# Layer 0's offset stage: depthwise convolution in four 64x64 tiles, with the channel mean folded into its weights

## Chip, cores and metric

The kernel runs on one NeuronCore of a Trainium2 chip. The metric is the time of one execution on the device, in microseconds. Before the change the median of three runs is 1776.24 us (1775.21 to 1776.89).

## What is computed

The reference applies four layers to x (4 images, 64 channels, 48 x 48 pixels), each to a normalised x and added back to x. The change touches the first part of the first layer (the change's short title calls it layer 1, the code calls it layer 0), a deformable convolution:

```python
x_proj = x_nhwc @ w_in + b_in
x1 = conv_general_dilated(x, dw_w, ..., feature_group_count=C)      # 3x3, depthwise
x1 = x1.transpose(0, 2, 3, 1) + dw_b
mu = x1.mean(-1, keepdims=True)
var = ((x1 - mu) ** 2).mean(-1, keepdims=True)
x1 = (x1 - mu) * jax.lax.rsqrt(var + EPS) * ln_g + ln_b
x1 = jax.nn.gelu(x1, approximate=False)
offset = x1 @ w_off + b_off
mask = softmax((x1 @ w_mask + b_mask).reshape(N, H, W, G, P))
```

Mean and variance run over the 64 channels of one pixel. The stage that is changed, `offsets0`, makes `x_proj` and the raw offsets and mask values (`om`, 108 columns per pixel). What follows it in the kernel starts only when all of it is there.

## The kernel before

x lies in SBUF with 128 partitions: the lower 64 are the channels of images 0 and 1, the upper 64 those of images 2 and 3; the columns are two images side by side (`b2` is 0 or 1). `xp` is the same with a border of zeros. A chunk is 8 rows of 48 pixels, 384 columns, in both halves of the partitions at once, so the stage has 12 chunks (6 for each `b2`).

`vector_setup` (L142 to L164) runs ahead of the stage. VectorE makes `dwdiag` there (L154): for each of the nine taps a 128x128 diagonal matrix of the depthwise weights.

`offsets0` (L231 to L329) is a block in which each engine follows its own queue and waits on semaphores. For one chunk:

- TensorE: nine matmuls of 128x128 by 384 columns (L255), one for each tap, accumulate the convolution in one PSUM bank. In float32 each matmul is recorded as two passes. Then the channel mean (L264) and the channel mean of the squares (L268), both by a matmul with `halfm` (1/64 in each 64x64 diagonal block), the projection x_proj (L272), and three matmuls of 216 columns, one for each 128 pixels, that make the offsets and mask values (L277).
- ScalarE: adds the bias (L293), squares (L296), takes the root (L298), applies the gelu (L300) and moves the projection out with its bias (L305). Before some of them it loads an activation table.
- VectorE: subtracts the mean (L316), takes the reciprocal of the root (L318), multiplies (L319) and adds the bias of the offsets (L321).
- GpSimd: one memset of the projection's buffer at the start (L329).

The order on TensorE is written out by hand: mean of chunk n, taps 0 to 2 of chunk n + 1, variance of n, taps 3 to 8 of n + 1, projection of n, offsets of n. The chunks run in loops. There is one buffer for each intermediate, in SBUF and in PSUM.

Two other places of the kernel have a part in what follows. `dynamic3`, the last layer, has a 3x3 convolution in four 64x64 tiles with 384 columns (L1921), written as `for t in range(TAPS): for h, c in four:` with `four = [(h, c) for h in range(2) for c in range(2)]`; h is the half of the input partitions and picks the PSUM bank, c is one of two neighbouring chunks and picks the half of the PSUM partitions. `windows1`, in the second layer, has such a convolution with 192 columns (L1227) between matmuls of other shapes (L1173, L1193).

Of the kernel before, what the change touches and what calls it, by code (L numbers as in the profile page):

```python
# [22 lines left out]
TAPS = 9  # L23
G = 4
ROWS = 8
CH = ROWS * WW
CPI = HH // ROWS
TPC = CH // PT
# [3 lines left out]
OM = 3 * MG  # L32
# [5 lines left out]
VC = {n: i for i, n in enumerate(V64)}  # L38
# [186 lines left out]
def chunk_window(xp, b2, r, tap):  # L225

    dy, dx = divmod(tap, 3)
    return xp[:, b2, bass.ds(r * ROWS + dy, ROWS), dx:dx + WW]


def offsets0(nc, k, om):  # L231

    ctx, ps, xp, xn = k["ctx"], k["psum"], k["xp"], k["xn"]
    big = k["work0"]
    conv, cent, sq, root, inv, z, gel, xs = (big[:, CH * i:CH * i + CH] for i in range(8))
    xq = k["xproj"]
    S = {n: signal(k, "off0_" + n) for n in
         ("conv_ps", "conv", "mean_ps", "cent", "sq", "var_ps", "root", "z", "gelu", "om_ps", "om",
          "proj_ps", "proj", "steps", "cleared")}
    p_conv, p_mean, p_var = ps[:, 0:CH], ps[:, 512:512 + CH], ps[:, 1024:1024 + CH]  # L240
    p_om = ps[:, 1536:1536 + TPC * 256].rearrange("p (t n) -> p t n", t=TPC)
    p_proj = ps[:, 2560:2560 + CH]
    vec = k["vec"]

    def turns(eng):
        for b2 in range(2):
            with eng.Fori(0, CPI) as r:
                yield b2, r, b2 * CPI + r + 1

    with nc.Block() as block:  # L250
        @block.tensor
        def _(pe):
            def taps(b2, r, which):
                for t in which:
                    mm = pe.matmul(p_conv.rearrange("p (y x) -> p y x", y=ROWS), k["dwdiag"][:, t, :],  # L255
                                   chunk_window(xp, b2, r, t), start=(t == 0), stop=(t == TAPS - 1))
                if t == TAPS - 1:
                    mm.then_inc(S["conv_ps"], 1)

            def chunk(b2, r, after):  # L260

                n = b2 * CPI + r + 1
                pe.wait_ge(S["conv"], n)
                pe.matmul(p_mean, k["halfm"][:, :], conv, start=True, stop=True).then_inc(S["mean_ps"], 1)  # L264
                if after:
                    taps(*after, range(3))
                pe.wait_ge(S["sq"], n)
                pe.matmul(p_var, k["halfm"][:, :], sq, start=True, stop=True).then_inc(S["var_ps"], 1)  # L268
                if after:
                    taps(*after, range(3, TAPS))  # L270
                pe.wait_ge(S["proj"], n)
                pe.matmul(p_proj, k["win"][:, :], xn[:, bass.ds(r * CH + b2 * PIX, CH)], start=True, stop=True)\  # L272
                    .then_inc(S["proj_ps"], 1)
                pe.wait_ge(S["gelu"], n)
                pe.wait_ge(S["om"], n)
                for t in range(TPC):
                    mm = pe.matmul(p_om[:, t, 0:2 * OM], gel[:, PT * t:PT * t + PT], k["wom"][:, :],  # L277
                                   start=True, stop=True)
                mm.then_inc(S["om_ps"], 1)

            pe.sem_inc(S["om"], 1)
            pe.sem_inc(S["proj"], 1)
            taps(0, 0, range(TAPS))
            for b2 in range(2):
                with pe.Fori(0, CPI - 1) as r:
                    chunk(b2, r, (b2, r + 1))
                chunk(b2, CPI - 1, None if b2 else (1, 0))

        @block.scalar
        def _(act):  # L290
            for b2, r, n in turns(act):
                act.wait_ge(S["conv_ps"], n)
                act.activation(conv, p_conv, ACT.Identity, bias=vec[:, VC["dw_b"]:VC["dw_b"] + 1])\  # L293
                    .then_inc(S["conv"], 1)
                act.wait_ge(S["cent"], n)
                act.activation(sq, cent, ACT.Square).then_inc(S["sq"], 1)  # L296
                act.wait_ge(S["var_ps"], n)
                act.activation(root, p_var, ACT.Sqrt, bias=k["eps"][:, 0:1]).then_inc(S["root"], 1)  # L298
                act.wait_ge(S["z"], n)
                act.activation(gel, z, ACT.Gelu, scale=vec[:, VC["ln_g"]:VC["ln_g"] + 1],  # L300
                               bias=vec[:, VC["ln_b"]:VC["ln_b"] + 1]).then_inc(S["gelu"], 1)
                if b2 == 0:
                    act.wait_ge(S["cleared"], 1)
                act.wait_ge(S["proj_ps"], n)
                act.activation(xq[:, b2, bass.ds(r * ROWS + 2, ROWS), 2:2 + WW],  # L305
                               p_proj.rearrange("p (y x) -> p y x", y=ROWS), ACT.Identity,
                               bias=vec[:, VC["b_in"]:VC["b_in"] + 1]).then_inc(S["proj"], 1)

        @block.vector
        def _(v):  # L310
            step = Chain(v, S["steps"])
            for b2 in range(2):
                with v.Fori(0, CPI) as r, step.body(r, 1, CPI):
                    n = b2 * CPI + r + 1
                    v.wait_ge(S["mean_ps"], n)
# [4 lines left out]
                    v.wait_ge(S["om_ps"], n)  # L320
                    v.tensor_tensor(om[:, bass.ds((r + b2 * CPI) * (2 * TPC), 2 * TPC), :]  # L321
                                    .rearrange("p (t h) n -> p t h n", h=2),
                                    p_om[:, :, 0:2 * OM].rearrange("p t (h n) -> p t h n", h=2),
                                    k["b_om"][:, :].unsqueeze(1).unsqueeze(1).to_broadcast([128, TPC, 2, OM]),
                                    ALU.add).then_inc(S["om"], 1)
# [1658 lines left out]
def program(nc, dram):  # L1984
    with ExitStack() as ctx:
        k = {"ctx": ctx, "dram": dram, "nc": nc, "signals": []}
# [31 lines left out]
        AR = 33000  # L2018
        arena = sb("arena", [128, AR])[:, :]
        k["arena"] = arena  # L2020
        k["dwdiag"] = arena[:, 15000:15000 + TAPS * 128].rearrange("p (t n) -> p t n", t=TAPS)
# [17 lines left out]
        with nc.If(wide < WIDE):  # L2039

            n = M * 2 * MG
            at = M * OM
# [5 lines left out]
            n = NT * 3 * 2 * G * W * W // 2  # L2048
# [32 lines left out]
        at = M * NO1 + 6 * CH  # L2081
# [5 lines left out]
        at = size + 2 * PIX  # L2087
# [4 lines left out]
        win = [window_slot(at)]  # L2092
# [22 lines left out]
        xn = k["xn"]  # L2115
# [9 lines left out]
        with nc.Else():  # L2125

            turn_offsets1(nc, k, raw, om1, work1)
            at = AR - M * NO1
# [155 lines left out]
```

## Time and profile before

| | |
|---|---|
| median of three runs | 1776.24 us |
| profiled execution | 1776.49 us |
| its span on the core | 1774.7 us |
| mean granted clock of TensorE | 0.889 of full speed |
| the stage `offsets0` | from 50 us to 179.5 us of the span |

The span is the time from the first to the last instruction of the profiled execution; 1.8 us of its time lie around it. Start times in the rows count from the span's start. PE is TensorE's matmuls, PEld its weight loads, DVE is VectorE, ACT ScalarE, POOL GpSimd. A row with idle time names what ended it. A merged row of matmuls covers the time from the first one's start to the last one's end, and ends of matmuls are modelled; matmuls overlap, so the mean duration of one is longer than the time between the starts of two.

### The profile page before, as it was taken

The numbers are of one execution on the slowest core, as the hardware profiler recorded it, in microseconds if no ns is written. First come the engines' busy times: TensorE is split into PE (matmuls) and PEld (weight loads), VectorE is DVE, ScalarE is ACT, GpSimd is POOL, SyncE is SP. The second block draws the span as 40 slices with busy tenths as digits, with TensorE's granted clock in tenths as the row PEclk, the third lists the DMA queues.
The fourth block names the chain that finished last, engine by engine and source line by source line (L and its number), as shares of the span: only waits on it lengthen the run. The fifth ranks groups of instructions, "written<-read, shape, count | busy, mean of one in ns | idle before, by whom it ended". The sixth has DMA issues, their size and how long they took to land. (4 is left out here: it accounts for less than half of the span.)

```text
span 1774.7 us, 29960 instructions
## 1 busy us (share of the span) xinstructions
PE 1353.8 (76%) x11778; PEld 638.7 (36%) x11778; DVE 1011.3 (57%) x1203; ACT 782.4 (44%) x1089; POOL 634.1 (36%) x374
## 2 busy tenths in 40 slices
PE   0798001888818589999999999558999999999548
PEld 0455000555413234444444445332333333333123
DVE  1344897989833745555555554568455655553333
ACT  2465205332133446666666666261344444445230
POOL 1100141999902200000000000020788888889700
PEclk9999555999957779999999999775899999999869
DMA  4000000000011000001000100010000000000033
GB/s 80 2 0 0 0 0 0 1 0 0 0 43 40 23 12 24 24 23 35 24 24 24 35 24 13 1 37 17 1 2 2 1 1 2 1 2 2 9 111 61
DMA packets 28472, 31.17 MB, mean 18 GB/s; under 512 B 18900, under 2 KB 21389, under 8 KB 27709
## 3 DMA queue, kind: packets, MB, share of 16 engines
q1 hardware_dynamic: 28349, 29.43, 6.7%
q8 instruction: 89, 1.46, 0.3%
q14 instruction: 34, 0.28, 0.1%
HBM read 21.08 MB, written 5.35 MB: 15 GB/s over the span
## 5 line engine op out<-in xcount | busy, mean ns | idle before, releaser
L1780 POOL TENSOR_TENSOR arena_sb<-arena_sb 128x768 f32<-128x768 f32 x204 | 375.3, 1840 | 115.5 <-ACT arena_sb L1741 91.7
L1302 DVE TENSOR_TENSOR arena_sb<-ps,arena_sb 120x768 f32<-120x768 f32 x216 | 206.8, 957 | 186.7 <-ACT arena_sb L1263 186.0
L1741 ACT ACTIVATE arena_sb<-ps 128x768 f32<-128x768 f32 x216 | 175.0, 811 | 272.6 <-PE ps L1672 249.7
L1792 DVE TENSOR_REDUCE arena_sb<-ps 128x4 f32<-128x1536 f32 x108 | 188.5, 1753 | 167.1 <-PE ps L1641 165.9
L1263 ACT ACTIVATE arena_sb<-ps 120x768 f32<-120x768 f32 x216 | 175.2, 811 | 154.4 <-PE ps L1193 154.4
L1193 PE MATMUL ps<-xp_sb,arena_sb 32*120 32x384 f32 x1728 | 206.9, 549 | 22.4 <-ACT arena_sb L1263 7.4
L1485 POOL MEMSET arena_sb<- 128x64 f32 x1 | 0.2, 152 | 567.9 <-POOLq L182 567.9
L1672 PE MATMUL ps<-arena_sb 33*64 33x384 f32 x1728 | 187.1, 502 | 15.7 <-ACT arena_sb L1741 9.3
L1211 PE MATMUL ps<-arena_sb 120*64 120x216 f32 x1536 | 182.4, 359 | 0.0
L1684 PE MATMUL ps<-arena_sb 64*64 64x384 f32 x1728 | 169.1, 487 | 1.9 <-ACT arena_sb L1741 1.5
L579 DVE TENSOR_TENSOR arena_sb<-ps,arena_sb 128x384 f32<-128x384 f32 x300 | 143.3, 547 | 20.7 <-PE ps L546 19.8
L1211 PEld LDWEIGHTS ps<-arena_sb 120*64 120x64 f32 x1536 | 93.3, 136 | 119.8 <-ACT xp_sb L1270 89.6
L489 POOL TENSOR_TENSOR arena_sb<-arena_sb 128x768 f32<-128x768 f32 x60 | 112.4, 1874 | 40.0 <-DVE arena_sb L579 40.0
L1641 PE MATMUL ps<-arena_sb 32*128 32x384 f32 x864 | 115.6, 611 | 13.3 <-DVE arena_sb L1792 9.8
L528 PE MATMUL ps<-identb_sb,arena_sb 128*120 128x128 bf16 x180 | 23.4, 240 | 118.3 <-PEq L557 117.8
L1270 ACT ACTIVATE xp_sb<-ps 128x432 f32<-128x432 f32 x192 | 102.1, 532 | 15.5 <-PE ps L1211 6.3
L1193 PEld LDWEIGHTS ps<-xp_sb,arena_sb 32*120 32x120 f32 x1728 | 67.4, 182 | 110.1 <-ACT arena_sb L1263 99.5
L1672 PEld LDWEIGHTS ps<-arena_sb 33*64 33x64 f32 x1728 | 55.1, 133 | 120.8 <-ACT arena_sb L1741 102.6
L1684 PEld LDWEIGHTS ps<-arena_sb 64*64 64x64 f32 x1728 | 65.3, 134 | 80.0 <-issue 68.4
L255 PE MATMUL ps<-xp_sb,arena_sb 128*128 (+1 forms) x216 | 75.2, 494 | 24.0 <-PEq L143 24.0
L1227 PE MATMUL ps<-xp_sb,arena_sb 64*64 64x192 f32 x1728 | 80.8, 328 | 0.8 <-ACT xp_sb L1270 0.6
L536 PE MATMUL ps<-arena_sb,wout_sb 128*128 128x384 f32 x120 | 54.2, 534 | 22.1 <-ACT arena_sb L506 11.6
(211 smaller groups left out, 1710.7 us busy)
## 6 DMA issues: line engine op xcount, KB each, us to landing
arena_sb<-pixel_major SPq DMA_DIRECT2D x96, 120.0 KB, 2.3
arena_sb<-in_W SPq DMA_DIRECT2D x1, 4608.0 KB, 13.7
pixel_major<-arena_sb SPq DMA_DIRECT2D x24, 108.0 KB
x_sb<-in_x SPq DMA_DIRECT2D x4, 576.0 KB, 8.6
arena_sb<-arena_sb SPq DMA_DIRECT2D x8, 288.0 KB, 5.4
out_x<-x_sb SPq DMA_DIRECT2D x24, 96.0 KB, 2.2
arena_sb<-arena_sb SPq DMA_DIRECT2D x16, 36.0 KB, 3.7
arena_sb<-arena_sb SPq DMA_DIRECT2D x24, 1.5 KB
```

The costliest lines, as they stand in the source:

```text
L489: pool.tensor_tensor(a, a, pr[:, (W * u + 2) * CH:(W * u + 4) * CH], ALU.add).then_inc(S["sum1"], 1)
L579: v_.tensor_tensor(prod[u][v].rearrange("p (y x) -> p y x", y=ROWS), p_b[v].rearrange("p (y x) -> p y x", y=ROWS), xq[:, b2, bass.ds(r * R ...
L1193: mm = pe.matmul(out, k["spr"][32 * row:32 * row + 32, q, :], hat[32 * row:32 * row + 32, slot, :], start=True, stop=True)
L1211: mm = pe.matmul(out[64 * v:64 * v + 64, :, :, IW * t:IW * t + IW], win[n % 2][0:KW, band, tile, :], weights[:, TAPS * v:TAPS * v + TAPS, ...
L1263: act.activation(xs[t % 2].rearrange("p (e n) -> p e n", e=2), p_x, ACT.Copy).then_inc(S["x_out"], 1)
L1302: v_.tensor_tensor(bmat[m % 2][:, 2 * CH * t:2 * CH * t + 2 * CH].rearrange("p (e n) -> p e n", e=2), p_y[t % 2], xs[t % 2].rearrange("p ( ...
L1641: mm = pe.matmul(p_m(m)[:, u, :], q4[own, CH * ib + PT * a:CH * ib + PT * a + PT], k4[own, CH * jc:CH * jc + CH], start=True, stop=True)
L1672: mm = pe.matmul(p_scores(g)[64 * i:64 * i + 64, h, :], kp[own, key:key + 64], qp[own, PIX * b2 + CH * ib:PIX * b2 + CH * ib + CH], start= ...
L1684: mm = pe.matmul(p_o[64 * h:64 * h + 64, i, :], at[64 * i:64 * i + 64, b2 * TPI + j, 64 * h:64 * h + 64], pt[g % SLOTS][64 * i:64 * i + 64 ...
L1741: act.activation(pt[g % SLOTS].rearrange("p (h n) -> p h n", h=2), p_scores(g), ACT.Exp)\
L1780: pool.tensor_tensor(acc, first, pt[g % SLOTS], ALU.add).then_inc(S["pool_added"], 1)
L1792: v.tensor_reduce(part.rearrange("p (a u j) -> p a u j", a=3, u=NB)[:, a, :, jc], p_m(m), AX.X, ALU.max)\
```

## The change

- The weights: `dwdiag` becomes nine matrices of 64 columns, made from `centre` (the 64x64 unit matrix in both halves, less 1/64) in place of the unit matrix. A matmul with them gives the convolution less its mean over the channels.
- Two chunks of the same image pair form a pair, six pairs in all. For each tap there are four matmuls with 64 rows and 64 columns of weights: h is the half of the input partitions (and the PSUM bank), c the chunk of the pair (and the half of the PSUM partitions). The convolution has two sets of two banks.
- The matmul for the mean, the bias step on ScalarE and the subtraction on VectorE go. The bias less its own mean, `cb`, is made once by a small matmul and one VectorE operation; it is the bias of the square, and VectorE adds it as it multiplies by the reciprocal, straight from PSUM.
- Square and root work on 768 columns at once. Reciprocal, product, gelu, offsets and bias of the offsets go by half h, 384 pixels, as before. Variance and projection share one pair of banks.
- The order on TensorE for pair n is: taps 0 and 1 of pair n + 1, variance of n, offsets of the lower half of n - 1, taps 2 to 4 of n + 1, projection of n, offsets of the upper half of n - 1, taps 5 to 8 of n + 1. VectorE does the offsets' bias of n - 1, lower half, before the reciprocals of n, and that of the upper half after them.
- The loops are unrolled on all engines.

```diff
+            step(v.tensor_scalar(k["centre"], k["stack2"][:, :], 1.0 / C, None, ALU.subtract))
             for t in range(TAPS):
-                v.tensor_scalar(k["dwdiag"][:, t, :], k["ident"][:, :], k["dw"][:, t:t + 1], None, ALU.mult)
+                v.tensor_scalar(k["dwdiag"][:, t, :], k["centre"], k["dw"][:, t:t + 1], None, ALU.mult)
...
-            def taps(b2, r, which):
+            def taps(n, which):
+                b2, i = divmod(n, NP)
+                if which[0] == 0 and n >= 2:
+                    pe.wait_ge(S["z"], 2 * (n - 1))
                 for t in which:
-                    mm = pe.matmul(p_conv.rearrange("p (y x) -> p y x", y=ROWS), k["dwdiag"][:, t, :],
-                                   chunk_window(xp, b2, r, t), start=(t == 0), stop=(t == TAPS - 1))
+                    dy, dx = divmod(t, 3)
+                    for h in range(2):
+                        own = slice(64 * h, 64 * h + 64)
+                        for c in range(2):
+                            y0 = (2 * i + c) * ROWS + dy
+                            mm = pe.matmul(p_conv[n % 2][64 * c:64 * c + 64, h, :].rearrange("p (y x) -> p y x", y=ROWS),
+                                           k["dwdiag"][own, t, :], xp[own, b2, y0:y0 + ROWS, dx:dx + WW],
+                                           start=(t == 0), stop=(t == TAPS - 1), skip_group_check=True)
...
+            def variance(n):
+                pe.wait_ge(S["sq"], n + 1)
+                if n:
+                    pe.wait_ge(S["proj"], n)
+                for h in range(2):
+                    mm = pe.matmul(p_var[:, h, :], k["halfm"][:, :], sq[:, h, :], start=True, stop=True)
+                mm.then_inc(S["var_ps"], 1)
...
+            def offsets(n, h):
+                pe.wait_ge(S["gelu"], 2 * n + h + 1)
+                if n or h:
+                    pe.wait_ge(S["om"], 2 * n + h)
...
+            for n in range(PAIRS):
+                more = n + 1 < PAIRS
+                if more:
+                    taps(n + 1, range(0, 2))
+                variance(n)
+                if n:
+                    offsets(n - 1, 0)
+                if more:
+                    taps(n + 1, range(2, 5))
+                project(n)
+                if n:
+                    offsets(n - 1, 1)
+                if more:
+                    taps(n + 1, range(5, TAPS))
+            offsets(PAIRS - 1, 0)
+            offsets(PAIRS - 1, 1)
...
-                act.activation(conv, p_conv, ACT.Identity, bias=vec[:, VC["dw_b"]:VC["dw_b"] + 1])\
-                    .then_inc(S["conv"], 1)
...
+            act.wait_ge(S["bias"], 1)
+            for n in range(PAIRS):
+                b2, i = divmod(n, NP)
+                act.wait_ge(S["conv_ps"], n + 1)
+                if n:
+                    act.wait_ge(S["var_ps"], n)
+                act.activation(sq, p_conv[n % 2], ACT.Square, bias=cb).then_inc(S["sq"], 1)
+                act.wait_ge(S["var_ps"], n + 1)
+                if n:
+                    act.wait_ge(S["z"], 2 * n)
+                act.activation(inv, p_var, ACT.Sqrt, bias=k["eps"][:, 0:1]).then_inc(S["root"], 1)
...
-                    v.tensor_tensor(cent, conv, p_mean, ALU.subtract).then_inc(S["cent"], 1)
-                    v.wait_ge(S["root"], n)
-                    step(v.reciprocal(inv, root))
-                    v.tensor_tensor(z, cent, inv, ALU.mult).then_inc(S["z"], 1)
...
+            for n in range(PAIRS):
+                if n:
+                    offsets(n - 1, 0)
+                v.wait_ge(S["root"], n + 1)
+                for h in range(2):
+                    v.reciprocal(inv[:, h, :], inv[:, h, :]).then_inc(S["inv"], 1)
+                    if n:
+                        v.wait_ge(S["gelu"], 2 * n + h - 1)
+                    v.wait_ge(S["inv"], 2 * n + h + 1)
+                    v.scalar_tensor_tensor(z[:, h, :], p_conv[n % 2][:, h, :], cb, inv[:, h, :], ALU.add, ALU.mult)\
+                        .then_inc(S["z"], 1)
+                if n:
+                    offsets(n - 1, 1)
+            offsets(PAIRS - 1, 0)
+            offsets(PAIRS - 1, 1)
```

## Rows read from the trace of the kernel before

**Rows 1.** Stretches, the two loops: length, busy PE, PEld, DVE, ACT, POOL, PEclk, DMA.
```profile
58.67:123.24 64.57, 57.55 (x185) 33.82 (x186) 27.32 (x25) 39.55 (x47) 0.00 (x0) 1.00 0.00 0
123.24:179.60 56.36, 49.30 (x159) 29.10 (x157) 26.09 (x24) 31.99 (x41) 0.00 (x0) 0.97 0.00 0
```
**Rows 2.** Timeline, second loop: start us, us, what, idle before it and its releaser.
```profile
158.91 0.91 PE L264 MATMUL ps<-arena_sb,halfm_sb 128*128 128x384 f32 x2
...
162.24 4.03 PE L255 MATMUL ps<-xp_sb,arena_sb 128*128 x12
...
166.11 0.81 PE L272 MATMUL ps<-xn_sb,win_sb 128*128 x2
166.99 1.36 PE L277 MATMUL ps<-wom_sb,arena_sb 128*128 128x216 f32 x6
168.19 0.91 PE L264 MATMUL ps<-arena_sb,halfm_sb 128*128 128x384 f32 x2
168.52 0.83 DVE L321 TENSOR_TENSOR arena_sb<-ps,b_om_sb 128x648 f32 x1 [2.33 <-PE ps L277]
```
**Rows 3.** Groups of the stage, by line: busy us, mean ns of one, idle before.
```profile
L318 DVE RECIPROCAL arena_sb<-arena_sb 128x384 f32<-128x384 f32 x12 | 30.6, 2553 | 30.9 <-ACT arena_sb L298 30.9
L298 ACT ACT_TABLE_LOAD x12 | 15.4, 1283 | 0.2
L300 ACT ACT_TABLE_LOAD x12 | 15.4, 1283 | 0.2
L293 ACT ACT_TABLE_LOAD x6 | 7.7, 1283 | 3.3 <-PEq L143 3.2
L321 DVE TENSOR_TENSOR arena_sb<-ps,b_om_sb 128x648 f32 x12 | 10.0, 832 | 28.8 <-PE ps L277 28.8
L300 ACT ACTIVATE arena_sb<-arena_sb,vec_sb 128x384 f32<-128x384 f32 x12 | 8.5, 706 | 23.0 <-DVE arena_sb L319 23.0
L305 ACT ACTIVATE arena_sb<-ps,vec_sb 128x384 f32 x12 | 7.0, 582 | 1.9 <-PE ps L272 1.2
L319 DVE TENSOR_TENSOR arena_sb<-arena_sb 128x384 f32<-128x384 f32 x12 | 6.7, 558 | 0.4
```
**Rows 4.** Timeline, the last layer's tiled convolution.
```profile
1732.80 36.84 PE L1921 MATMUL ps<-xp_sb,arena_sb 64*64 64x384 f32 x432 [9.87 <-DVE arena_sb L1952]
...
1752.06 0.14 PEld L1921 LDWEIGHTS ps<-xp_sb,arena_sb 64*64 64x64 f32 x4 [0.18 <-issue]
...
1752.38 0.14 PEld L1921 LDWEIGHTS ps<-xp_sb,arena_sb 64*64 64x64 f32 x4 [0.18 <-issue]
```
**Rows 5.** Timeline, second layer: matmuls of unlike tile shapes in turn.
```profile
799.82 1.21 PE L1227 MATMUL ps<-xp_sb,arena_sb 64*64 64x192 f32 x24
800.96 0.50 PE L1173 MATMUL ps<-arena_sb 109*128 109x384 bf16 x2
801.39 2.18 PE L1227 MATMUL ps<-xp_sb,arena_sb 64*64 64x192 f32 x48
803.50 0.60 PE L1193 MATMUL ps<-xp_sb,arena_sb 32*120 32x384 f32 x4
```
**Rows 6.** The page's costliest groups, 768 columns on ScalarE.
```profile
L1741 ACT ACTIVATE arena_sb<-ps 128x768 f32<-128x768 f32 x216 | 175.0, 811 | 272.6 <-PE ps L1672 249.7
```
**Rows 7.** Timeline, the stage's beginning and end.
```profile
46.70 1.85 DVE L154 TENSOR_SCALAR arena_sb<-ident_sb,dw_sb 128x128 f32<-128x128 f32 x9
48.46 0.16 DVE L160 RECIPROCAL bn_sb<-bn_sb 128x1 f32<-128x1 f32 x1
...
50.28 7.72 PE L255 MATMUL ps<-xp_sb,arena_sb 128*128 128x384 f32 x18 [24.01 <-PEq L143]
...
176.24 2.26 PE L277 MATMUL ps<-wom_sb,arena_sb 128*128 128x216 f32 x6 [4.26 <-ACT arena_sb L300]
178.67 0.83 DVE L321 TENSOR_TENSOR arena_sb<-ps,b_om_sb 128x648 f32 x1 [3.23 <-PE ps L277]
179.84 5.55 DVE L340 TENSOR_REDUCE small_sb<-arena_sb 128x1 f32<-128x5184 f32 x1 [0.34 <-PEq L250]
```

More of the change, by code:

```diff
@@ L231, in offsets0, with pair @@
 def offsets0(nc, k, om):
-    ctx, ps, xp, xn = k["ctx"], k["psum"], k["xp"], k["xn"]
+    ps, xp, xn, vec = k["psum"], k["xp"], k["xn"], k["vec"]
     big = k["work0"]
-    conv, cent, sq, root, inv, z, gel, xs = (big[:, CH * i:CH * i + CH] for i in range(8))
-    xq = k["xproj"]
+    sq, inv, z, gel = (big[:, 2 * CH * i:2 * CH * i + 2 * CH].rearrange("p (h n) -> p h n", h=2) for i in range(4))
+    xq, cb = k["xproj"], k["small"][:, 2:3]
     S = {n: signal(k, "off0_" + n) for n in
[L238 to L248, printed above, removed]
+         ("bias_ps", "bias", "conv_ps", "sq", "var_ps", "root", "inv", "z", "gelu", "om_ps", "om", "proj_ps", "proj",
+          "cleared")}
+    def pair(at):
+        return ps[:, at:at + 1024].rearrange("p (h n) -> p h n", h=2)[:, :, 0:CH]
+    p_conv, p_var = [pair(0), pair(1024)], pair(2048)
+    p_om = ps[:, 3072:3072 + 256 * TPC].rearrange("p (t n) -> p t n", t=TPC)
+    omv = om.rearrange("p (q c t h) n -> p q c t h n", c=2, t=TPC, h=2)
+    NP = CPI // 2
+    PAIRS = 2 * NP
     with nc.Block() as block:
@@ L260, in chunk @@
[L260 to L275, printed above, removed]
+                    dy, dx = divmod(t, 3)
@@ new lines, in taps, with project @@
+                if which[-1] == TAPS - 1:
+                    mm.then_inc(S["conv_ps"], 1)
+            def variance(n):
[5 more added lines that the diff above has]
+                mm.then_inc(S["var_ps"], 1)
+            def project(n):
+                b2, i = divmod(n, NP)
+                pe.wait_ge(S["root"], n + 1)
+                for c in range(2):
+                    at = PIX * b2 + CH * (2 * i + c)
+                    mm = pe.matmul(p_var[:, c, :], k["win"][:, :], xn[:, at:at + CH], start=True, stop=True)
+                mm.then_inc(S["proj_ps"], 1)
@@ L282, in _ @@
[L282 to L287, printed above, removed]
+            pe.matmul(ps[:, 2048:2050], k["halfm"][:, :], vec[:, VC["dw_b"]:VC["dw_b"] + 2], start=True, stop=True)\
+                .then_inc(S["bias_ps"], 1)
+            taps(0, range(TAPS))
+            for n in range(PAIRS):
[12 more added lines that the diff above has]
+                    taps(n + 1, range(5, TAPS))
@@ new lines, in _ @@
+            act.wait_ge(S["bias"], 1)
+            for n in range(PAIRS):
+                b2, i = divmod(n, NP)
+                act.wait_ge(S["conv_ps"], n + 1)
[6 more added lines that the diff above has]
+                act.activation(inv, p_var, ACT.Sqrt, bias=k["eps"][:, 0:1]).then_inc(S["root"], 1)
+                if n == 0:
+                    act.wait_ge(S["cleared"], 1)
+                act.wait_ge(S["proj_ps"], n + 1)
+                for c in range(2):
+                    y0 = (2 * i + c) * ROWS + 2
+                    last = act.activation(xq[:, b2, y0:y0 + ROWS, 2:2 + WW],
+                                          p_var[:, c, :].rearrange("p (y x) -> p y x", y=ROWS), ACT.Identity,
+                                          bias=vec[:, VC["b_in"]:VC["b_in"] + 1])
+                last.then_inc(S["proj"], 1)
+                for h in range(2):
+                    act.wait_ge(S["z"], 2 * n + h + 1)
+                    if n:
+                        act.wait_ge(S["om_ps"], 2 * n + h - 1)
+                    act.activation(gel[:, h, :], z[:, h, :], ACT.Gelu, scale=vec[:, VC["ln_g"]:VC["ln_g"] + 1],
+                                   bias=vec[:, VC["ln_b"]:VC["ln_b"] + 1]).then_inc(S["gelu"], 1)
@@ L309, in _, with offsets @@
         @block.vector
         def _(v):
[L311 to L315, printed above, removed]
-                    v.tensor_tensor(cent, conv, p_mean, ALU.subtract).then_inc(S["cent"], 1)
-                    v.wait_ge(S["root"], n)
-                    step(v.reciprocal(inv, root))
-                    v.tensor_tensor(z, cent, inv, ALU.mult).then_inc(S["z"], 1)
[L320 to L325, printed above, removed]
+            def offsets(n, h):
+                v.wait_ge(S["om_ps"], 2 * n + h + 1)
+                v.tensor_tensor(omv[:, n, :, :, h, :], p_om[:, :, 0:2 * OM].rearrange("p t (c n) -> p c t n", c=2),
+                                k["b_om"][:, :].unsqueeze(1).unsqueeze(1).to_broadcast([128, 2, TPC, OM]), ALU.add)\
+                    .then_inc(S["om"], 1)
@@ new lines, in _ @@
+            v.wait_ge(S["bias_ps"], 1)
+            v.tensor_tensor(cb, vec[:, VC["dw_b"]:VC["dw_b"] + 1], ps[:, 2048:2049], ALU.subtract).then_inc(S["bias"], 1)
+            v.wait_ge(S["bias"], 1)
+            for n in range(PAIRS):
+                if n:
+                    offsets(n - 1, 0)
+                v.wait_ge(S["root"], n + 1)
+                for h in range(2):
+                    v.reciprocal(inv[:, h, :], inv[:, h, :]).then_inc(S["inv"], 1)
[4 more added lines that the diff above has]
+                        .then_inc(S["z"], 1)
+                if n:
+                    offsets(n - 1, 1)
@@ L2020, in program @@
         k["arena"] = arena
-        k["dwdiag"] = arena[:, 15000:15000 + TAPS * 128].rearrange("p (t n) -> p t n", t=TAPS)
+        k["dwdiag"] = arena[:, 15000:15000 + TAPS * C].rearrange("p (t n) -> p t n", t=TAPS)
+        k["centre"] = arena[:, 15000 + TAPS * C:15000 + TAPS * C + C]
         k["psum"] = ctx.enter_context(nc.psum_tensor("ps", [128, 4096], F32))[:, :]
```

18 lines of the change are left out of this document (1 added, 17 removed).

## Prediction

> **What bounds the kernel now.** The whole kernel is a row of stages that hardly overlap, so the page's shares say little here; I cut out the stage and read the busy time by stretch first. In the loop of the second images TensorE is busy 49.3 of 56.4 us, VectorE 26.1 and ScalarE 32.0; in the loop of the first images TensorE is busy 57.6 of 64.6 us [rows 1]. TensorE is the bound, and the timeline shows how closely. One chunk of the second loop takes 168.19 - 158.91 = 9.28 us [rows 2]. Twelve passes of 384 columns take 166.11 - 162.24 = 3.87 us, 0.322 us each [rows 2]. A chunk has 18 passes for the taps and 6 for mean, variance and projection, 24 x 0.322 = 7.73 us, and six passes of 216 columns for the offsets, which hold TensorE for 168.19 - 166.99 = 1.20 us [rows 2]. That is 8.9 of 9.28 us. The first loop is 1.5 us slower per chunk (64.57 / 6 = 10.76), nearly one more table load: L293 loads a table six times, 1.28 us each, while the other two loads come twelve times [rows 3].
>
> The stage's own end matters in full: the next block's first operation, a reduction over all offsets, starts at 179.84 us, 0.34 us after the last VectorE operation of the stage ended [rows 7]. What the stage loses, the kernel loses.
>
> **TensorE's new work.** The taps go in four 64x64 tiles. The trace has this very loop in the last layer: same order of h and c, same 384 columns, 432 passes, which is also the number here (6 pairs x 9 taps x 4 tiles x 2 passes). Weight loads come there in fours, 1752.38 - 1752.06 = 0.32 us apart, and all 432 passes lie in 36.84 us with the slow start in it [rows 4]. So one pass costs 0.0805 us, and the taps of a pair 72 x 0.0805 = 5.80 us, where two chunks paid 11.6. Mean passes go (4 x 0.322 = 1.29 us per pair). Variance and projection stay at 8 x 0.322 = 2.58 us, offsets at 2 x 1.20 = 2.40.
>
> New is that 64x64 and 128x128 matmuls alternate, four times per pair. From the 192-column tiles (0.040 us each): 24 take 0.96 us and the next shape starts after 1.14, 48 take 1.92 and it starts after 2.11; the two 384-column passes between take 0.43 for 0.32 [rows 5]. So leaving the tiles costs 0.18, entering them 0.11, and a pair pays 0.58 us. Together a pair asks 5.80 + 2.58 + 2.40 + 0.58 = 11.4 us of TensorE against 18.6 to 21.5 before.
>
> **The others' new work, per pair.** VectorE: two reciprocals of 2.55, two products of 0.56, two offset adds of 0.83 [rows 3], 7.9 us. The product now reads PSUM and adds a column's scalar; no row shows that form. From below it could cost nothing more than 0.55, from above twice that; I take 0.56, its two-operand neighbour of the same size. ScalarE: square and root of 768 columns at 0.81 each [rows 6], two projections at 0.58, two gelus at 0.71, and table loads. By the rows gelu and root are the two operations that always load [rows 3], so I count two, 2.57 us; the third in the first loop stands at its head and goes with the loop. Sum 6.8 us.
>
> **The chain.** Each of the two has room within 11.4 us, but they wait for one another. I follow one period from the moment E at which the variance passes of pair n end on TensorE.
> - TensorE makes the offsets of n - 1, lower half. VectorE sees such a group 168.52 - 166.99 = 1.53 us after its start [rows 2]; 0.1 of it was a weight load behind a wait, which isn't there now: E + 1.43. VectorE's next item in its queue is that add, 0.83, and only behind it stand the reciprocals: E + 2.3. The root of n is ready 0.2 + 0.81 after E and off the chain.
> - Reciprocal, product, twice: 2 x (2.55 + 0.56) + 0.17 of steps between = 6.39: E + 8.7.
> - Gelu of the upper half 0.71, and behind it in ScalarE's queue the square of n + 1, 0.81, with steps of 0.1: E + 10.3. The product's end also frees the PSUM banks for taps 0 and 1 of n + 2, which take 1.29 us and a switch; they end just about then.
> - Variance of n + 1: 0.05 + 1.29 + 0.1 for weights that are loaded only after the wait.
>
> That is 11.7 us a period. TensorE's demand of 11.4 and this chain nearly agree: were the chain free, a period would be 0.3 shorter.
>
> **The sum.** Taps of pair 0 start at 50.3, cold as before: 7.7 us for the same column time [rows 7], 0.3 for the bias matmul ahead. Then taps 0 and 1 of pair 1 (1.3), the switch, variance 1.3: E0 = 61.0. The first period has no offsets in front, so the root (E + 1.1) opens it in place of E + 2.3: 10.5 us. Four periods of 11.7 bring E5 to 118.3. The tail: VectorE adds the offsets of pair 4, upper half, only after both products, done at E5 + 9.5, and both offset groups of pair 5 wait for that one PSUM buffer. By then TensorE has been idle for some 6 us. Before, the last six passes came after 4.26 us idle and took 178.67 - 176.24 = 2.43 us until VectorE could start, the slower level of the clock [rows 7]. So twice 2.43 + 0.83, with steps 6.6: the stage ends at 118.3 + 16.1 = 134.4, where it ended at 179.5. Saved: 45.1 us.
>
> The weights ahead of it: nine operations in 1.85 us, 0.206 each; a one-column one takes 0.16 [rows 7]. Halving 128 columns saves 0.02 to 0.03 each, the added `centre` costs some 0.2: nothing. If the operations scaled fully it would be a gain of 0.7.
>
> Against its own time of 1776.49 that gives 1731.4; the median is 0.25 lower, so **1731.1 us**.
>
> **Rivals.**
> - *The tiles overlap two at a time*, since both passes of one tile come one after the other. Then a pass is worth 0.161 and a period 11.6 + 2.58 + 2.40 + 0.58 = 17.2, all TensorE's. E0 is 50.6 + 1.7 of cold start + 88 x 0.161 + 1.5 = 68; E5 is 68 + 5 x 17.2 less 5 for the offsets missing in the first period and the taps missing in the last, 149; the end 165: 14.5 us saved, 1762. The last layer's rows speak against it. 5 in 100.
> - *The tiles don't overlap at all where they share rows* (slower). The order puts c inside h, so four passes in a row read the same 64 partitions. Each pass then pays up to 0.322, a period 23.2 + 5.6 = 28.8, the end comes at 82 + 5 x 28.8 - 7.5 + 16 = 234.5: plus 55, 1831. By the same sum it breaks even with before where a pass costs 0.20 us. Rows 4 have the same order at 0.0805, which is what speaks against it; for it, only that no other shape stands between them there. 2 in 100.
>   The Trainium skill (TensorE: Matmul & The Clock Gate, Part 3, The mechanism) says that a weight load overlaps a running matmul only if their row groups differ; here it would stand bare in most passes. The trace contradicts: four loads per 0.32 us beside matmuls that never pause.
> - *The clock is granted at 1.2 GHz through the stage*. Periods become 2 x 10.8 + 0.58 = 22.1, E0 is 67.6, E5 171, the end 187: plus 7.5, 1784. Against it: the granted clock was 1.00 through the first loop with TensorE idle 11% of the time [rows 1], and in my chain TensorE's gaps stay under 0.5 us. 3 in 100.
> - *One more table load per pair* on the chain, ahead of the square, 1.28 each: 6 us, 1737.5. 10 in 100.
>
> **How the numbers follow.** The rest, 80 in 100, is the forecast with its own errors: switches twice as dear (+3), the product or the square 0.2 off (1 each per period, five times), a period of 11.4 if the waits close up (-1.5), or of 11.1 if the weights of the offsets' passes load faster than in rows 2 (-3), fetching unrolled code (a few us). That and the table loads give 1723 to 1742, which leaves out the first three rivals. Two tenths of a per cent, 3.5 us, is about what a measurement of this kernel can tell from nothing. Faster by more 0.95, within it 0.01, slower 0.04.
>
> **What would show it.** Right: 432 tap passes in place of 216, at 0.08 us each; variance passes 11 to 12 us apart; 12 table loads or so; VectorE's reciprocal after the offset add, not after the root; next stage at about 134 us, all later stages as long as before. Wrong: passes in steps of 0.16 or 0.32, PEclk under 1 between 60 and 118 us, or waits of TensorE over 1 us in each period.

## The result and the profile after

The changed kernel takes 1729.62 us in the median of four runs (1728.52 to 1730.97), against 1775.83 us for the kernel before (four runs). The ratio is 0.974, its 95% interval 0.9723 to 0.9756. Forecast were 1731.1 us, range 1723 to 1742.

The profiled execution took 1729.56 us, its span is 1727.8 us, 46.9 less than before. The stage has the following timeline, from the variance of pair 4 to the next block's first operation. Its columns are those of [rows 2]: start us, duration us, engine, line, operation, operands and count, then idle time before it and what ended it. Here and below, weight loads, table loads and rows that the text does not use are left out of the timelines.

```profile
104.69 1.56 PE L275 MATMUL ps<-arena_sb,halfm_sb 128*128 128x384 f32 x4
106.09 1.26 PE L291 MATMUL ps<-wom_sb,arena_sb 128*128 128x216 f32 x6
106.29 0.90 ACT L327 ACTIVATE arena_sb<-ps,eps_sb 128x768 f32<-128x768 f32 x1 [0.35 <-PE ps L275]
107.28 2.17 PE L264 MATMUL ps<-xp_sb,arena_sb 64*64 64x384 f32 x24
107.38 0.83 DVE L348 TENSOR_TENSOR arena_sb<-ps,b_om_sb 128x648 f32<-128x648 f32 x1 [3.54 <-PE ps L291]
108.13 2.54 DVE L360 RECIPROCAL arena_sb<-arena_sb 128x384 f32<-128x384 f32 x1
109.37 1.56 PE L283 MATMUL ps<-xn_sb,win_sb 128*128 128x384 f32 x4
110.77 1.26 PE L291 MATMUL ps<-wom_sb,arena_sb 128*128 128x216 f32 x6
110.78 0.62 DVE L364 SCALAR_TENSOR_TENSOR arena_sb<-ps,small_sb,arena_sb 128x384 f32<-128x384 f32 x1
111.31 2.54 DVE L360 RECIPROCAL arena_sb<-arena_sb 128x384 f32<-128x384 f32 x1
113.96 0.62 DVE L364 SCALAR_TENSOR_TENSOR arena_sb<-ps,small_sb,arena_sb 128x384 f32<-128x384 f32 x1
114.61 0.71 ACT L341 ACTIVATE arena_sb<-arena_sb,vec_sb 128x384 f32<-128x384 f32 x1 [0.57 <-DVE arena_sb L364]
115.22 0.88 ACT L323 ACTIVATE arena_sb<-ps,small_sb 128x768 f32<-128x768 f32 x1
116.16 1.56 PE L275 MATMUL ps<-arena_sb,halfm_sb 128*128 128x384 f32 x4 [1.39 <-ACT arena_sb L323]
...
125.96 0.82 DVE L348 TENSOR_TENSOR arena_sb<-ps,b_om_sb 128x648 f32<-128x648 f32 x1
126.93 2.50 PE L291 MATMUL ps<-wom_sb,arena_sb 128*128 128x216 f32 x6 [5.57 <-ACT arena_sb L341]
129.46 0.83 DVE L348 TENSOR_TENSOR arena_sb<-ps,b_om_sb 128x648 f32<-128x648 f32 x1 [2.68 <-PE ps L291]
130.44 2.50 PE L291 MATMUL ps<-wom_sb,arena_sb 128*128 128x216 f32 x6 [1.02 <-DVE arena_sb L348]
132.98 0.83 DVE L348 TENSOR_TENSOR arena_sb<-ps,b_om_sb 128x648 f32<-128x648 f32 x1 [2.68 <-PE ps L291]
134.14 5.55 DVE L384 TENSOR_REDUCE small_sb<-arena_sb 128x1 f32<-128x5184 f32 x1 [0.33 <-PEq L251]
```

Read it against [rows 2] and [rows 7]. The variance passes of two pairs lie 116.16 - 104.69 = 11.47 us apart, where two chunks of the second loop took 2 x 9.28. The reduction that opens the next block starts at 134.14 us; it started at 179.84. So the stage gives 45.70 us of the span's 46.9.

The groups of the stage, by line: busy us, mean ns of one, idle before and its releaser. They answer to [rows 3] and [rows 4].

```profile
L264 PE MATMUL ps<-xp_sb,arena_sb 64*64 64x384 f32 x432 | 39.9, 510 | 1.1 <-DVE arena_sb L364 1.1
L360 DVE RECIPROCAL arena_sb<-arena_sb 128x384 f32<-128x384 f32 x12 | 30.5, 2543 | 11.6 <-ACT arena_sb L327 11.6
L341 ACT ACT_TABLE_LOAD x6 | 7.7, 1283 | 0.1
L327 ACT ACT_TABLE_LOAD x5 | 6.4, 1283 | 0.1
```

The 432 tap passes cover 39.9 us; before, 216 full ones at 0.322 us took about 70. Table loads are eleven in place of thirty (12, 12 and 6 in [rows 3]). TensorE's one wait of over 1 us for the product lies in the first period. VectorE waits for the root only once, 11.6 us ahead of the first reciprocal; in all later pairs the reciprocal follows the offset add without a wait. The clock by stretch (length, busy time of PE, PEld, DVE, ACT, POOL, granted clock, DMA share, GB/s) answers to [rows 1]:

```profile
60.00:120.00 60.00, 57.49 (x446) 29.85 (x446) 38.30 (x30) 34.52 (x41) 0.00 (x0) 1.00 0.00 1
120.00:134.00 14.00, 6.36 (x19) 4.62 (x17) 8.24 (x7) 3.75 (x5) 0.00 (x0) 0.72 0.00 0
```

TensorE is still busy 96% of the loop, at full clock. In the tail it mostly waits, and the granted clock is 0.72 there.

### The profile page after: what moved, and what is told of

Read it like the earlier page. It is cut to its first block and busy times, and to the rows that moved or that the text cites. A ratio compares the mean times of both kernels' runs of the same rounds, so it can differ in the third digit from the quotient of the medians.

```text
span 1727.8 us, 30092 instructions
## 1 busy us (share of the span) xinstructions
PE 1310.9 (76%) x11972; PEld 608.9 (35%) x11972; DVE 1006.0 (58%) x1193; ACT 748.2 (43%) x1046; POOL 633.9 (37%) x374
## 5 line engine op out<-in xcount | busy, mean ns | idle before, releaser
L580 PE MATMUL ps<-arena_sb,wout_sb 128*128 128x384 f32 x120 | 54.2, 534 | 21.6 <-ACT arena_sb L550 11.4
L1685 PEld LDWEIGHTS ps<-arena_sb 32*128 32x128 f32 x864 | 37.7, 203 | 88.4 <-issue 46.5
```

Of the source, the lines that this page charges most:

```text
L1685: mm = pe.matmul(p_m(m)[:, u, :], q4[own, CH * ib + PT * a:CH * ib + PT * a + PT], k4[own, CH * jc:CH * jc + CH], start=True, stop=True)
```

## Experiments

In the expectations the "chain" is the round of waits from variance through offsets, add, reciprocals, products, gelu and square to the next variance. Totals stand beside a median of the kernel before of 1775.56 us (e1 to e4) and 1775.07 us (e9 to e12). e5 to e9 were run once and are read by their traces. Each experiment is judged by two readings of its trace, which leave out the scatter of the rest of the kernel: the distance of two variance groups, and the start of the next block.

### What each part of the change is worth

**e1: the tiles undone.**

```diff
-                    for h in range(2):
-                        own = slice(64 * h, 64 * h + 64)
-                        for c in range(2):
...
-                            mm = pe.matmul(p_conv[n % 2][64 * c:64 * c + 64, h, :]..., k["dwdiag"][own, t, :],
+                    for c in range(2):
...
+                        mm = pe.matmul(p_conv[n % 2][:, c, :]..., k["dwdiag"][:, t, :],
+                                       xp[:, b2, y0:y0 + ROWS, dx:dx + WW], ...)
```

> The changed kernel with its tiles undone: per tap two matmuls of 128x128 by 384 columns, one for each chunk of the pair, with centred block-diagonal weights; mean folded, pairs, order, buffers and unrolling stay. Theory (the gain of the tiles is TensorE's time): TensorE's demand per pair becomes 36 x 0.322 + 2.58 + 2.38 = 16.6 us, above the waiting chain's 11.5, so periods of 16.6 us, the stage ends at about 162, total about 1758 (28 us above the changed kernel, 17 below the kernel before). Rival (the gain comes from the folded mean, the pairs and the double buffers, and TensorE was not what held the old stage back): the period stays at 11.5 to 13 and the total within 8 us of 1730.

Measured: 1759.99 us, ratio 0.9922 (0.9905 to 0.9938). The timeline of its TensorE and of what waits for it:

```profile
97.48 1.45 PE L273 MATMUL ps<-arena_sb,halfm_sb 128*128 128x384 f32 x4
98.77 1.26 PE L289 MATMUL ps<-wom_sb,arena_sb 128*128 128x216 f32 x6
99.86 4.04 PE L262 MATMUL ps<-xp_sb,arena_sb 128*128 128x384 f32 x12
103.74 1.45 PE L281 MATMUL ps<-xn_sb,win_sb 128*128 128x384 f32 x4
105.03 1.26 PE L289 MATMUL ps<-wom_sb,arena_sb 128*128 128x216 f32 x6
106.12 6.29 PE L262 MATMUL ps<-xp_sb,arena_sb 128*128 128x384 f32 x19
111.48 0.90 ACT L321 ACTIVATE arena_sb<-ps,small_sb 128x768 f32<-128x768 f32 x1 [2.58 <-PE ps L262]
```

In a period TensorE is never idle between groups, while ScalarE waits 2.58 us for the taps (the window ends inside the last group of taps, which has 24 passes). The next variance is at 113.86: periods of 113.86 - 97.48 = 16.4 us, and the next block starts at 163.2. The tiles alone are worth 163.2 - 134.1 = 29.1 us, and nearly all of it is TensorE's time; 0.5 us is a later start (50.57 against 50.06), as the weights made ahead of the stage are twice as wide. The rival falls.

**e2: the mean folded, nothing else.**

```diff
-                pe.matmul(p_mean, k["halfm"][:, :], conv, start=True, stop=True).then_inc(S["mean_ps"], 1)
...
-                act.activation(conv, p_conv, ACT.Identity, bias=vec[:, VC["dw_b"]:VC["dw_b"] + 1])\
+                act.activation(conv, p_conv, ACT.Identity, bias=cb)\
                     .then_inc(S["conv"], 1)
-                act.wait_ge(S["cent"], n)
-                act.activation(sq, cent, ACT.Square).then_inc(S["sq"], 1)
+                act.wait_ge(S["conv"], n)
+                act.activation(sq, conv, ACT.Square).then_inc(S["sq"], 1)
...
-                    v.tensor_tensor(cent, conv, p_mean, ALU.subtract).then_inc(S["cent"], 1)
```

> The kernel before with only the mean folded into 128x128 weights: the mean matmul and VectorE's subtraction go, the bias less its mean is made once. Loops, single buffers and full-array taps stay. Theory: in the second loop TensorE bounds and loses 2 x 0.322 us of 9.28, so chunks of 8.65; in the first loop the chain through the third table load bounds and loses the mean matmul with its wait and the subtraction, 1.6 us of 10.76, so chunks of 9.1. Together -14 us, about 1762. Rival (the chain bounds both loops alike): -1.6 x 12 = -19, about 1757. Rival (only TensorE counts): -0.64 x 12 = -8, about 1768.

Measured: 1771.13 us, ratio 0.998 (0.997 to 0.9989); the next block starts at 174.4, only 5.4 us earlier. The second loop's chunks take 8.75 us, as expected (8.65), the first loop's 10.2 and not 9.1. Its timeline says why:

```profile
90.65 0.58 ACT L297 ACTIVATE arena_sb<-ps,small_sb 128x384 f32<-128x384 f32 x1
91.27 0.52 ACT L300 ACTIVATE arena_sb<-arena_sb 128x384 f32<-128x384 f32 x1
91.39 2.20 PE L257 MATMUL ps<-xp_sb,arena_sb 128*128 x6 [1.41 <-ACT arena_sb L297]
93.42 0.81 PE L269 MATMUL ps<-arena_sb,halfm_sb 128*128 128x384 f32 x2
94.27 0.58 ACT L302 ACTIVATE arena_sb<-ps,eps_sb 128x384 f32<-128x384 f32 x1 [1.18 <-PE ps L269]
```

The square is ready at 91.79. But on TensorE three taps (six passes) stand ahead of the variance, and they wait for the one convolution buffer to be emptied. So the variance starts 1.63 us after its square is ready, and the root waits 1.18 us for TensorE. Before, the mean's round trip covered all but 0.6 us of these taps (square ready at 71.50, variance at 72.13); with the mean gone the order written by hand bares them. My expectation had followed the chain and not the queue in which one of its links stands. That is 5 x 1.1 us of the 8.6 that are missing from the expected 14. Another 1.1 is the sixth chunk, which was never a slow one, and 1.4 lie at the start: one more operation and a matmul stand ahead of the taps, and more of their first passes take 0.64 us each, so the first variance comes at 62.78 and not at 61.36.

**e3: the loops unrolled, nothing else.**

```diff
-            with eng.Fori(0, CPI) as r:
+            for r in range(CPI):
...
-                with pe.Fori(0, CPI - 1) as r:
+                for r in range(CPI - 1):
```

> The kernel before with its loops unrolled and nothing else. Theory: the table load at the head of the first loop goes, its six chunks fall from 10.76 to 9.28 us, -9 us, about 1767. Rival (the third table load is needed by the operation and not by the loop, or it was hidden): no change, 1776. A cost of fetching more instructions would show as chunks above 9.3 us.

Measured: 1769.31 us, ratio 0.9962 (0.9951 to 0.9972). The chunks of both loops take 9.2 us (in the first loop, mean matmuls at 77.46 and 86.67), the table load before the bias step is gone, and the next block starts at 171.9, 7.9 us earlier. I had counted six long chunks; only the five steps from one turn of the first loop to the next carry the load, since the first load of all lies beside the first taps. The price of the longer code is not to be seen.

Together: unrolling gives 7.9 us of the stage and folding 5.4, each alone. Both, with the pairs and the second convolution buffer, give 179.8 - 163.2 = 16.6 (e1), so 3.3 us belong to the pairs, the buffer and the parts helping each other, the queue that spoils e2 among them; the runs do not separate these. The tiles give 29.1.

### What sets the period of 11.47 us

**e5: 0.8 us more on the chain, none on TensorE.**

```diff
                 v.wait_ge(S["om_ps"], 2 * n + h + 1)
+                if h == 0 and n + 1 < PAIRS:
+                    v.tensor_tensor(spare..., p_om[:, :, 0:2 * OM]..., k["b_om"]..., ALU.add)
```

> The changed kernel, with VectorE's add of the offsets of pair n - 1, lower half, done twice (the first into unused memory), which puts 0.8 us more ahead of the reciprocals and nothing on TensorE. Theory (the waiting chain variance, offsets, add, reciprocals, gelu, square sets the period of 11.47 us, with TensorE's own 11.29 just under it): periods of 12.2 to 12.3 us, stage end 3.5 to 4 later. Rival (TensorE alone bounds; the chain has room): period 11.5, stage end under 1 us later.

Measured: variance at 94.01 and 106.21, periods of 12.2 us; the next block at 137.1, 3.0 later. The chain carries the addition almost in full (0.73 of the 0.75 by which two adds follow each other). The stage's end moved less than the expected 3.5 to 4, since only four periods carry it: 4 x 0.73 = 2.9.

**e6: one more offsets group on TensorE, nothing on the chain.**

```diff
-                for t in range(TPC):
+                for t in [*range(TPC)] * (2 if h else 1):
```

> The changed kernel, with the three offsets matmuls of the upper half issued twice, writing the same values: 1.19 us more of TensorE per pair, and nothing on the chain before the reciprocals. Theory (TensorE's demand of 11.29 is only 0.2 below the period): 11.29 + 1.19 = 12.5 us a period, +4 over four periods, and about 2.4 more in the tail, where the last group runs doubled at the slow clock; stage end 6 to 7 us later. Rival (the chain alone bounds and TensorE has room): period 11.5, only the tail's 2.4.

Measured: variance at 83.81, 96.20, 108.59: periods of 12.39 us, next block at 140.3, 6.2 later.

```profile
102.27 2.35 PE L291 MATMUL ps<-wom_sb,arena_sb 128*128 128x216 f32 x12
104.56 4.10 PE L264 MATMUL ps<-xp_sb,arena_sb 64*64 64x384 f32 x48
```

Twelve passes hold TensorE for 104.56 - 102.27 = 2.29 us where six hold it for 1.19, so the extra ones cost 1.10 and not the 1.19 of the expectation. No group waits in these periods, so TensorE's own demand without them is 12.39 - 1.10 = 11.29 us, and it had 11.47 - 11.29 = 0.18 us of room. The chain sets the period, with TensorE that little below it; neither rival holds.

**e7: the add after the first product.**

```diff
-                if n:
-                    offsets(n - 1, 0)
                 v.wait_ge(S["root"], n + 1)
...
                         .then_inc(S["z"], 1)
+                    if n and h == 0:
+                        offsets(n - 1, 0)
```

> The changed kernel, with VectorE's add of the offsets of pair n - 1, lower half, moved from before the first reciprocal of pair n to behind the first product. The chain to the second product gets 0.1 us shorter, but TensorE's offsets of the upper half wait for this add: it would end near 88.35 where they now start at 87.83. Theory (both sides nearly bind): TensorE stalls 0.5 us a period, periods of 11.8 to 11.9. Rival (the order on VectorE is what costs, TensorE has room): periods of 11.3 to 11.4.

Measured: periods of 11.98 us, a little above the expected 11.8 to 11.9; next block at 136.4, 2.3 later. The wait is where it was expected:

```profile
100.12 0.82 DVE L348 TENSOR_TENSOR arena_sb<-ps,b_om_sb 128x648 f32<-128x648 f32 x1
101.09 1.33 PE L291 MATMUL ps<-wom_sb,arena_sb 128*128 128x216 f32 x6 [0.45 <-DVE arena_sb L348]
```

**e10: the square ahead of the second gelu.**

```diff
                 for h in range(2):
+                    if h and n + 1 < PAIRS:
+                        square(n + 1)
                     act.wait_ge(S["z"], 2 * n + h + 1)
```

> The changed kernel with ScalarE's square of pair n + 1 ahead of the gelu of the upper half of pair n. The chain from the second product no longer passes that gelu, 0.6 us shorter. Theory (TensorE's own 11.29 us is just under the period, so taking the chain away gives only the rest): periods of 11.3 to 11.4, total about 0.5 to 1 us less, hard to tell from nothing in the runs. Rival (the chain alone bounds): periods of 10.9.

Measured: periods of 11.39 us (variance at 93.27 and 104.66), next block at 133.7, 0.4 earlier. The total is 1732.21 us with an unusual scatter (1728.56 to 1738.03), ratio 0.9761 (0.9737 to 0.9785): not to be told from the changed kernel. With the gelu off the chain a period loses 0.08 us and no more, because TensorE has another wait at the same place: taps 0 and 1 of the next pair but one wait for the second product, and the variance stands behind them. In the trace the product ends at 91.76, the weights of these taps load from 91.81, and the variance starts at 93.27, though its square was ready at 92.91.

### Tiles, rows and order

**e8 and e9: two other orders of the four tiles.**

```diff
-                for t in which:
-                    dy, dx = divmod(t, 3)
-                    for h in range(2):
-                        own = slice(64 * h, 64 * h + 64)
+                for h in range(2):
+                    own = slice(64 * h, 64 * h + 64)
+                    for t in which:
+                        dy, dx = divmod(t, 3)
                         for c in range(2):
```

> The changed kernel with the order of the tiles turned: within each group of taps all matmuls of half h = 0 come first, then all of h = 1, so that only two of the four tiles are in turn at a time, both fed from the same 64 partitions. Theory (a pass of a tile takes its 0.322 us and neighbours in the queue overlap only if they are in other tiles): two at a time, 0.161 us a pass, periods of about 17 us, stage end about 163. Rival (tiles that share rows do not overlap): 0.322 us a pass, periods of 28.5. Rival (the order does not matter): 11.5.

```diff
-                    for h in range(2):
-                        own = slice(64 * h, 64 * h + 64)
-                        for c in range(2):
+                    for c in range(2):
+                        for h in range(2):
+                            own = slice(64 * h, 64 * h + 64)
```

> The changed kernel with the four tiles of a tap in the order c outside, h inside, so that neighbouring matmuls read different halves of the partitions (before, neighbours of one half shared them). Theory (four different tiles in turn overlap in full, whatever rows they share): 0.0805 us a pass as before, periods of 11.47. Rival (sharing rows with the neighbour costs something, as a weight load that waits): shorter tap groups, 24 passes in under 2.10 us.

e9 measured the same as the changed kernel: variance at 81.51 and 92.98 (11.47), next block at 133.9, 1729.22 us. e8 measured 13.33 us a period, next block at 150.6, 1744.65 us. Its theory (17) missed, and so did its last rival (11.5); the truth lies between them. Weight loads in a group of 24 passes show what happens. First the changed kernel, then e8:

```profile
84.33 0.21 PEld L264 LDWEIGHTS ps<-xp_sb,arena_sb 64*64 64x64 f32 x8 [0.27 <-issue]
84.71 0.15 PEld L264 LDWEIGHTS ps<-xp_sb,arena_sb 64*64 64x64 f32 x4 [0.17 <-issue]
85.03 0.15 PEld L264 LDWEIGHTS ps<-xp_sb,arena_sb 64*64 64x64 f32 x4 [0.17 <-issue]
```

```profile
95.42 0.19 PEld L264 LDWEIGHTS ps<-xp_sb,arena_sb 64*64 64x64 f32 x4 [0.27 <-issue]
95.80 0.14 PEld L264 LDWEIGHTS ps<-xp_sb,arena_sb 64*64 64x64 f32 x2 [0.18 <-issue]
96.12 0.85 PEld L264 LDWEIGHTS ps<-xp_sb,arena_sb 64*64 64x64 f32 x14 [0.18 <-issue]
97.16 0.14 PEld L264 LDWEIGHTS ps<-xp_sb,arena_sb 64*64 64x64 f32 x2 [0.18 <-issue]
97.48 0.14 PEld L264 LDWEIGHTS ps<-xp_sb,arena_sb 64*64 64x64 f32 x2 [0.18 <-issue]
```

With four tiles in turn, four loads go per 0.32 us. With two in turn, two loads go per 0.32 us at the start and the end of a group, which is the theory's 0.161 us a pass. But in the middle 14 loads go in 0.85 us. I read this as the second half's passes being let in beside the last ones of the first half; the rows do not say which half a load belongs to, so that is not shown. I had not expected it; it brings the 24 passes down to 98.22 - 95.43 = 2.79 us, where strict twos would need 24 x 0.161 = 3.87. How far the engine would reach ahead the runs do not settle.

### The tail

**e4: a second buffer for the last offsets but one.**

```diff
+    p_om2 = ps[:, 0:256 * TPC].rearrange("p (t n) -> p t n", t=TPC)
+
+    def om_bank(n, h):
+        return p_om2 if (n, h) == (PAIRS - 1, 0) else p_om
```

> The changed kernel, with the offsets matmuls of the last pair's lower half written to the PSUM banks of the convolution that are free by then, so that they don't wait for VectorE's add of pair 4. Theory (the 16 us after the last variance hold one buffer's serial waits at the slow clock): the lower group runs straight after its gelu, the upper one straight after the second gelu; stage end 3.5 to 4.5 us earlier (129.3 to 130.3), total about 1725.5. Rival (the tail is bound by reciprocal, product and gelu): under 1 us.

Measured: 1725.75 us, ratio 0.9729 (0.9713 to 0.9745); next block at 129.9, 4.2 us earlier.

```profile
122.94 1.36 PE L295 MATMUL ps<-wom_sb,arena_sb 128*128 128x216 f32 x6 [2.30 <-ACT arena_sb L345]
126.21 2.50 PE L295 MATMUL ps<-wom_sb,arena_sb 128*128 128x216 f32 x6 [1.91 <-ACT arena_sb L345]
```

The two groups are the same work. Before the first TensorE had been idle 2.30 us and it took 1.36; before the second 1.91 more, and it took 2.50. In this stretch the granted clock fell:

```profile
120.00:124.00 4.00, 1.70 (x10) 1.33 (x8) 3.90 (x3) 2.63 (x4) 0.00 (x0) 1.00 0.00 0
124.00:129.00 5.00, 2.80 (x8) 1.85 (x6) 2.95 (x5) 0.71 (x1) 0.00 (x0) 0.62 0.00 0
```

**e11: matmuls that keep the clock, on top of e4.**

```diff
+            pe.wait_ge(S["proj"], PAIRS)
+            keep_clock(3)
             offsets(PAIRS - 1, 0)
+            keep_clock(3)
             offsets(PAIRS - 1, 1)
```

> The kernel with the second offsets buffer in the tail, plus twice three matmuls of 384 columns into banks nobody reads any more, in the stretches where TensorE waits for the last two gelus. Theory (the last offsets group took 2.50 us and not 1.36 because the clock had fallen while TensorE waited): the last group at 1.3 to 1.6 us, stage end 0.9 to 1.1 us earlier than without them, near 128.9, total about 1724.8. Rival (the length is the group's own or the matmuls delay it): no change or later.

Measured: the same stretches at clock 1.00, the last group at full speed:

```profile
120.00:124.00 4.00, 3.91 (x16) 2.43 (x15) 3.90 (x3) 2.94 (x4) 0.00 (x0) 1.00 0.00 0
124.00:129.00 5.00, 3.86 (x16) 2.43 (x14) 3.85 (x5) 0.71 (x1) 0.00 (x0) 1.00 0.00 0
```

```profile
126.53 1.33 PE L295 MATMUL ps<-wom_sb,arena_sb 128*128 128x216 f32 x6
127.90 0.83 DVE L359 TENSOR_TENSOR arena_sb<-ps,b_om_sb 128x648 f32<-128x648 f32 x1 [0.78 <-PE ps L295]
```

The next block starts at 129.1, 0.85 us before e4's. In the total (1725.68 us, 1721.88 to 1726.36; ratio 0.9717, 0.9701 to 0.9733) this is not to be seen.

**e12: all three.** The edits of e4, e11 and e10 together.

> Second offsets buffer in the tail, matmuls that keep the clock there, and the square ahead of the gelu, together. Sum of the parts: -4.2, -1.0 and -0.5 to -0.8 us from the changed kernel's 1729.6, so 1723.7. Rival: the parts overlap in the last pair and give 1724.5 or more.

Measured: 1724.87 us (1722.76 to 1725.29), ratio 0.9715 (0.9702 to 0.9728); next block at 128.1. That is 6.0 us off the changed kernel's stage and 4.7 off its total. The five runs all lie below the changed kernel's four (1728.52 at the least), so it beats both kernels, though the two intervals of the ratios overlap. Its total is not to be told from e4's or e11's, whose runs overlap with it. The total lies above the forecast sum of 1723.7, while the stage gave all the parts promised. The rest of the kernel explains that.

### The rest of the kernel

From the start of the next block to the end of the span the untouched part takes 1774.7 - 179.84 = 1594.9 us before and 1727.8 - 134.14 = 1593.7 after. In the profiles of the other kernels it lies between 1592.2 (e8) and 1598.2 (e10), in no order that follows the stage: e3 has 1596.3, e4 1593.4, e12 1595.1. So the 1.2 us by which the span gained more than the stage are scatter of this size. The same holds for e10's profiled run (1733.76 us); its slowest run (1738.03) has no trace. Why the rest scatters so is open.

## Why the prediction was right

- *TensorE bound the old stage.* Shown by e1: with full-array taps the period goes to 16.4 us (16.6 by the rule of the prediction) although everything else stays as in the changed kernel.
- *A pass costs 0.0805 us.* 24 passes hold TensorE for 109.37 - 107.28 = 2.09 us, 1.93 and a switch of 0.16. The row of the last layer was the right one to take the price from, as it had the same shapes and the same order. The rivals "two at a time" and "not at all" are out; e8 shows that the first is real as soon as only two tiles are in turn.
- *Switches of 0.58 us a pair, offsets of 1.20.* Both were a little off, and the errors cancel, which is luck. e1 has the same groups with no switch between them: the variance holds TensorE for 98.77 - 97.48 = 1.29 us and the offsets for 99.86 - 98.77 = 1.09. In the changed kernel these are 106.09 - 104.69 = 1.40 and 107.28 - 106.09 = 1.19. So leaving the tiles costs 0.16 ahead of the next group and 0.11 within it, entering them costs 0.10, and a pair pays some 0.7 us. The 1.20 of [rows 2] held a weight load behind a wait, which the prediction took off VectorE's 1.53 and left in TensorE's term: the offsets' own price is 1.09. The sum was 11.4, measured are 11.29 (e6).
- *The chain of 11.7 us.* Measured 11.47. The first two steps were too long: VectorE starts its add 107.38 - 106.09 = 1.29 us after the offsets begin, not 1.43, and the reciprocal starts 0.75 after the add, not 0.83. The square takes 0.88, not 0.81, so the row of another function with 768 columns was a little short; the root takes 0.90 but is off the chain. The product that reads PSUM takes 0.62, not 0.56, though the next operation starts 0.53 after it began.
- *Chain and TensorE nearly agree.* Shown by e5 and e6 from both sides: the chain sets the 11.47, and TensorE alone would need 11.29. e10 removes a step of the chain and gains only 0.08; e7 makes TensorE wait for VectorE, and its period grows to 11.98.
- *First period, tail, slow clock.* E0 lies at 61.2 (61.0 forecast), the first period is 10.51 (10.5), the tail from E5 to the end 133.81 - 117.55 = 16.3 (16.1), with both last groups at 2.50 us after TensorE had waited. e4 and e11 show both parts of that reading, the buffer and the clock. The stage saved 45.7 us where 45.1 were forecast.
- *The clock in the loop.* It stayed at 1.00. The rival of 1.2 GHz is out.
- *Table loads.* Two a pair, eleven in all; the rival of one more per pair is out.
- *Fetching unrolled code (a few us, in the range).* No run shows this cost: the unrolled chunks of e3 take 9.2 us, where the second loop took 9.28.
- *The row-sharing rule.* The Trainium skill (TensorE: Matmul & The Clock Gate, Part 3, The mechanism) would have a weight load overlap a running matmul only where the row groups differ. The same section of the Trainium skill also has loads into a background weight buffer pulled ahead, which the prediction left out. Here four loads per 0.32 us go through an order in which four neighbouring passes share their rows, e9's order with alternating rows is not faster, and e8, with up to 16 passes in a row on the same rows, still overlaps two by two. In e1, where every pass uses all rows, the taps still follow at 0.32 us a pass (12 in 103.74 - 99.86 = 3.88 us). The measurement decides against the rule on row groups for this case.

The rest that was wrong was small. The prediction gave the first loop six slow chunks (64.57 / 6), but its window reached 1.4 us into the second loop; five is right, as e3 shows. Of the 1.8 us between the 1731.4 forecast for the profiled execution and its 1729.56, 0.6 come from the stage and 1.2 from the scatter of the rest, which no reasoning of the prediction covers.

## What to carry to other kernels

Look first for a price from the same shapes in the same order elsewhere in the same trace: here it held, while reasoning about how tiles overlap missed in e8. Check that the group a price comes from had no wait in it, as the offsets' 1.20 had. When a step leaves a chain, look at what stands in the queues ahead of the steps that remain: the mean's removal alone gave 5.4 us and not 14, for the most part since taps that waited for a buffer stood ahead of the variance. And in the tail of a stage, one buffer that serialises two groups and a clock that falls while TensorE waits cost 5 us here, which free banks and a few idle matmuls gave back.

## What was not expected of the hardware

- In the middle of e8's groups 14 weight loads go in 0.85 us, where the ends show two per 0.32 us: passes seem to be let in ahead of their place.
- A switch is paid in both directions. Leaving the tiles costs 0.16 us ahead of the next group and 0.11 within it; entering them makes the offsets ahead 1.19 us long instead of 1.09 (e1 against the changed kernel).
- An idle TensorE of 2.30 us left the next group at 1.36 us, 1.91 us more of idleness made it 2.50, with the granted clock at 0.62 over that stretch (e4).
